# Dense attention of the first layers: a look-ahead that builds up, softmax divisions in two parts, the value bias folded into the output bias, and another pace of the edge work

## What is computed

```python
num_heads = 4; head_dim = C // num_heads; scale = head_dim ** (-0.5); N = H * W
h = _group_norm(x, gn_gamma, gn_beta)
qkv = einsum('oc,bchw->bohw', qkv_w, h) + qkv_b[None, :, None, None]
q, k, v = split(qkv, 3, axis=1)              # each (B, num_heads, head_dim, N)
attn = softmax(einsum('bhdn,bhdm->bhnm', q, k) * scale, axis=-1)
out = einsum('bhnm,bhdm->bhdn', attn, v).reshape(B, C, H, W)
return x + einsum('oc,bchw->bohw', proj_w, out) + proj_b[None, :, None, None]
```

## Time and profile before

| | us |
|---|---|
| median of 3 runs | 2445.96 (2445.37 to 2446.14) |
| the profiled execution | 2440.69 |
| its span, first to last instruction | 2439.0 |
| PE busy, of the span | 1869.7 (77%) |
| DVE busy | 1559.3 (64%) |
| ACT busy | 1039.3 (43%) |
| POOL busy | 719.0 (29%) |
| mean granted TensorE clock | 0.841 of full speed |

### The profile page before, as it was taken

How to read it: one execution, slowest core, us unless ns; L and a number is a source line. 1 busy time by engine, 2 the same in 40 slices (tenths; PEclk the granted TensorE clock), 3 DMA queues, 4 the chain that set the end, 5 groups by cost and what they waited for, 6 DMA issues and landing times. The chain is left out here.

```text
span 2439.0 us, 26403 instructions
## 1 busy us (share of the span) xinstructions
PE 1869.7 (77%) x8810; PEld 846.6 (35%) x8810; DVE 1559.3 (64%) x3609; ACT 1039.3 (43%) x1724; POOL 719.0 (29%) x703
## 2 busy tenths in 40 slices
PE   2966995796688476689957888878878888978494
PEld 1213321321232134456631222222322324864264
DVE  4687777768777685556716575665566554635647
ACT  1333141233314116545533667657656653214255
POOL 3302600630270041024441322332322321127740
PEclk7878897888789787889966999989988986759797
DMA  7002100300120000021001111101011000014100
GB/s 197 1 21 59 44 2 25 77 17 20 50 52 3 25 1 1 1 102 21 14 30 51 42 31 40 41 17 40 29 29 38 3 5 15 1 54 62 10 7 35
DMA packets 55445, 80.16 MB, mean 33 GB/s; under 512 B 17249, under 2 KB 28504, under 8 KB 55073
## 3 DMA queue, kind: packets, MB, share of 16 engines
q1 hardware_dynamic: 44806, 69.14, 9.6%
q10 hardware_dynamic: 6426, 7.99, 1.5%
q0 software_dynamic: 4096, 1.58, 1.4%
HBM read 50.13 MB, written 24.68 MB: 31 GB/s over the span
## 5 line engine op out<-in xcount | busy, mean ns | idle before, releaser
L2460 DVE TENSOR_REDUCE f_half_max<-f_ring 128x1 f32<-128x512 f32 x512 | 334.9, 684 | 272.9 <-PE f_ring L2126 270.8
L2343 ACT ACTIVATE f_probs<-f_ST 128x512 f32<-128x512 f32 x512 | 293.0, 597 | 210.6 <-PE f_ST L2153 206.5
L2126 PE MATMUL f_ring<-f_stacks 96*128 96x512 bf16 x512 | 212.0, 415 | 54.5 <-DVE f_half_max L2460 28.1
L797 DVE TENSOR_REDUCE att_half_max<-att_ring 128x1 f32<-128x512 f32 x256 | 161.1, 683 | 88.1 <-PE att_ring L684 87.0
L2153 PE MATMUL f_ST<-f_stacks 99*128 99x512 bf16 x512 | 204.7, 405 | 10.3 <-ACT f_probs L2343 10.3
L780 ACT ACTIVATE att_probs<-att_ST 128x1024 f32<-128x1024 f32 x128 | 129.3, 1023 | 157.5 <-PE att_ST L709 157.3
L2170 PE MATMUL f_O<-f_probs,f_v_ext 128*32 128x512 f32 x1024 | 154.1, 677 | 0.1
L3182 POOL DMA_INDIRECT ti_row<-features,slot_from x128 | 127.9, 999 | 56.8 <-issue 56.8
L2126 PEld LDWEIGHTS f_ring<-f_stacks 96*128 96x128 bf16 x512 | 50.4, 99 | 258.8 <-DVE f_half_max L2460 162.6
L727 PE MATMUL att_O<-att_probs,v_ext 128*64 128x512 f32 x512 | 134.5, 652 | 6.4 <-DVE att_den L816 6.4
L709 PE MATMUL att_ST<-stacks 96*128 96x512 bf16 (+1 forms) x512 | 137.7, 397 | 0.0
(11 more groups left out here) (588 smaller groups left out, 3507.5 us busy)
## 6 DMA issues: line engine op xcount, KB each, us to landing
f_stacks<-f_parts SPq DMA_DIRECT2D x192, 64.0 KB, 2.2
parts_dram<-l_parts SPq DMA_DIRECT2D x8, 768.0 KB, 3.6
stacks<-parts_dram SPq DMA_DIRECT2D x24, 256.0 KB, 9.7
stacks<-parts_dram ACTq DMA_DIRECT2D x24, 256.0 KB, 10.8
f_parts<-f_parts SPq DMA_DIRECT2D x8, 768.0 KB, 3.5
es_raw<-L_ffn_edge_index SPq DMA_DIRECT2D x8, 512.0 KB, 4.6
bm_mix<-mix SPq DMA_DIRECT2D x8, 512.0 KB, 9.0
xn_cm<-x SPq DMA_DIRECT2D x4, 512.0 KB, 4.2
```

The source lines that it names most:

```text
L797: nc.vector.tensor_reduce(half_max[:, h % 2, t, n:n + 1], ring[:, i % RING], AX.X, ALU.max, negate=True).then_inc(reduced, 1)
L2126: nc.tensor.matmul(ring[:, i % RING], f.stacks[0:STACK, 0, at, t * P:(t + 1) * P], f.stacks[0:STACK, 1, at, n * BANK:(n + 1) * BANK], star ...
L2343: nc.scalar.activation(f.probs[:, s % PROBS, n * BANK:(n + 1) * BANK], ST[:, i % HALVES], ACT.Exp).then_inc(probs_ready, 1)
L2460: nc.vector.tensor_reduce(f.half_max[:, h % 2, t, n:n + 1], ring[:, i % RING], AX.X, ALU.max, negate=True).then_inc(reduced, 1)
```

## The change

In words, in the order of the code:

- `begin`: PE multiplies the output weights with the value bias (one column), and DVE adds the output bias to the result (`k.qb[:, 2:3]`). The sum takes the place of the output bias in the last operation of the attention, and ACT's addition of the value bias to `o_cm` goes.
- `schedule` in `dense_attention`: no scores of the next head at step 0, two tiles (4 products) at steps 1, 2 and 3, one tile from step 4. From step 3 on the same tiles have been made as before. The same in the fifth layer.
- `divide`: the three first heads are divided on 96 rows, in four operations (a reciprocal of one half, its product, the other half) that are taken one a step at steps 26 to 29, ahead of the edge work of that step.
- The last head: `carry_off(3)` goes on both engines. DVE takes one reciprocal of the whole output bank and multiplies 32 rows of numerators with it for either half. PE's output product waits for this alone.
- Edge work: two pieces a step from step 18 instead of from step 22; what would be left after the loop comes behind the last division instead of ahead of it.
- POOL's eight operations wait until the shift parts of head 0 are made.

```diff
@@ begin
+            pe.wait_ge(off, len(order))
+            nc.tensor.matmul(bank_of(0)[:, 0:1], k.turned[:, 3, :], k.cols[:, C_QKV_B + 2:C_QKV_B + 3], start=True,
+                             stop=True).then_inc(folded, 1)
...
+            dve.wait_ge(folded, 1)
+            link(nc.vector.tensor_tensor(k.qb[:, 2:3], bank_of(0)[:, 0:1], k.cols[:, C_PROJ_B:C_PROJ_B + 1], ALU.add))
@@ dense_attention (the same three lines of the schedule in fourth_layer_stream)
+    def ahead(s):
+        return max(min(s + AHEAD, 2 * (s - 1)), 0)
+
...
-        r = s + in_group + AHEAD
-        schedule(s, tiles(in_group if s == 0 else r, r + 1))
+        schedule(s, tiles(in_group + ahead(s), in_group + ahead(s + 1)))
...
+        inverse = c.enter_context(sbuf(nc, "att_inverse", [P, BANK], F32))
...
-                pe.wait_ge(biased, n + 1)
+                pe.wait_ge(normed, NC2 * (groups - 1) + n + 1)
                 nc.tensor.matmul(ring[:, n], w_out, chunk(o_cm, n), start=True, stop=True).then_inc(projected, 1)
...
-            carry_off(groups - 1)
-            for n in range(NC2):
-                act.wait_ge(normed, n + 1)
-                affine(nc, True, chunk(o_cm, n), chunk(o_cm, n), 1.0, bias).then_inc(biased, 1)
...
+            def divide(n):
+                link(nc.vector.reciprocal(den[0:32 * (groups - 1), n * BANK:(n + 1) * BANK],
+                                          den[0:32 * (groups - 1), n * BANK:(n + 1) * BANK]))
+                yield
+                dve.wait_ge(off_by_act, OFF_BY_ACT * (groups - 1))
+                x = o_cm[0:32 * (groups - 1), n * BANK:(n + 1) * BANK]
+                nc.vector.tensor_tensor(x, x, den[0:32 * (groups - 1), n * BANK:(n + 1) * BANK],
+                                        ALU.mult).then_inc(normed, groups - 1)
+                yield
+
+            division = itertools.chain(divide(0), divide(1))
...
+                if s > ends[groups - 2] + visit:
+                    if s == ends[groups - 2] + visit + 1:
+                        dve.wait_ge(off_by_dve, NC2 * (groups - 1))
+                    next(division, None)
                 if beside is not None and s >= EDGES_FROM:
-                    for _ in range(1 if s < in_group + AHEAD + EDGES_FROM - 2 else 2):
+                    for _ in range(1 if s < EDGES_FROM + 4 else 2):
                         next(edge_steps, None)
+            for _ in division:
+                pass
+            dve.wait_ge(mixed_ready, len(steps) // visit)
+            link(nc.vector.reciprocal(inverse[:], O[:]))
+            for n in range(NC2):
+                nc.vector.tensor_tensor(rows_of_group(o_cm, groups - 1, n), O[width * n:width * n + 32, :],
+                                        inverse[width * n + 32:width * (n + 1), :], ALU.mult).then_inc(normed, 1)
             if beside is not None:
                 for _ in edge_steps:
                     pass
-            if share == 1:
-                carry_off(groups - 1)
-                dve.wait_ge(off_by_dve, NC2 * groups)
...
-            for n in range(NC2):
-                link(nc.vector.reciprocal(chunk(den, n), chunk(den, n)))
-                if n == 0 and share == 1:
-                    dve.wait_ge(off_by_act, NC2 * groups)
-                nc.vector.tensor_tensor(chunk(o_cm, n), chunk(o_cm, n), chunk(den, n), ALU.mult).then_inc(normed, 1)
...
+                pool.wait_ge(parts_ready, 1)
                 beside.split(pool, edges_loaded, edges_linked, edges_coded)
@@ finish_attention
-                            chunk(x, n), bank, k.cols[:, C_PROJ_B:C_PROJ_B + 1],
+                            chunk(x, n), bank, k.qb[:, 2:3],
```

More of the change, by code:

```diff
@@ L1871, in fourth_layer_stream @@
     for s in range(len(steps)):
-        r = s + IN_GROUP + f.AHEAD
-        schedule(s, IN_GROUP if s == 0 else r, r + 1)
+        schedule(s, IN_GROUP + ahead(s), IN_GROUP + ahead(s + 1))
         if (s + 1) % NT == 0 and s + IN_GROUP < len(steps):
```

9 lines of the change are left out of this document (4 added, 5 removed).

## The result

The changed kernel takes 2472.3 us (median of 4 runs, 2468.1 to 2479.7), the kernel before 2445.7 (2444.6 to 2446.1): a ratio of 1.0114, 95% interval 1.0096 to 1.0132. It is slower, as forecast, but by 26.6 us instead of 9.0, and outside the range given (2443 to 2461).

A forecast was written before the change was run, and what follows sets the result against it. The limit was taken to change within an attention, DVE's queue setting its end; 9.6 (end) + 2.0 (start) - 2.2 (POOL's wait) - 0.4 (fifth layer) = +9.0 on 2445.96 gave 2455.0 us, range 2443 to 2461.

The forecast's parts named there:

- Part 1: End of each attention: a third reciprocal in DVE's queue outweighs what goes; 2.4 us later an image, +9.6 in all.
- rival 1: Output product: PE at full clock saves 2.0 us an image, giving 2447.1 us, not slower; chance 0.12.
- Part 2: Start of each attention: transposed products start 2.2 us earlier, but maxima gate the first mix; +0.5 an image, +2.0 in all.
- The upper bound: Start of each attention: +1.5 us an image if PE is still at its lower clock by the fourth step.
- Part 3: Head 0's shift parts: POOL's wait ends their collisions with POOL, saving 2.2 us in all.
- Rival 4: Head 1's shift parts: all five operations collide with POOL, +3.6 us an image, 2469 us; chance 0.05.
- Rival 3: Before the last mix: PE at the lower clock becomes the bound, 1 to 4 us an image, 2459 to 2471; chance 0.10.
- Rival 2: Start: maxima don't gate the first mix, so look-ahead gains 2.2 us each start, 2442.4 us; chance 0.13.
- Part 4: Rest: additions in `begin` hidden, folded bias free in the last operation, fifth layer's schedule edit between -2.2 and +1.5, middle -0.4.

The follow-up runs named there:

- the early pieces: Kernel before with folded bias, edge pieces at steps 6 to 29, one a step; with old division 2472.4 us, with new division 2463.2 us.
- the old pace: Changed kernel with edge pieces one a step until step 21 and two from step 22, the new division kept: 2482.4 us.
- the pause alone: Kernel before with folded bias, PE waiting until the first head's shift rows are off ACT before step 0's six scores: 2443.9 us, one execution.
- the pause filled: Changed kernel with two unused products before the first transposed product, 2466.8 us; or with two scores at step 0 instead of none, 2474.1 us.
- the filled pause: Changed kernel with two unused 512-column products between an image's first shift rows and its first transposed product: 2466.8 us.

## Why the prediction was right in sign and wrong in size

**The bill**, as sums over the four attentions of the profiled executions: before 458.1; the folded bias alone 456.2 (-1.9); on top of that the new ending 468.8 (+12.6), the look-ahead 468.1 (+11.9), both without POOL's wait 489.2 (+33.0, 8.5 more than the two by themselves, where three images lose more to head 0's parts and POOL); the whole change 482.7 (+24.6 over before). Cut at the maxima of step 18, 8.8 of the 24.6 lie behind them (forecast 9.6) and 15.8 ahead of them, where parts 2 and 3 had forecast -0.2.

**Part 1, the end: right.** Forecast 48.91 to 51.28 us from the maxima of step 18, +9.6 in all. In image 3 it is 842.61 - 791.41 = 51.20, the last reciprocal starts 833.90 - 791.41 = 42.49 behind those maxima (42.5 forecast), a reciprocal of 96 rows takes 3.35 and that of the output bank 3.36, DVE doesn't wait in between, and PE's last mix ends 3.9 us ahead in image 3 and 5.5 in the others (some 5 forecast). In images 0 to 2 the stretch is 50.9, 51.3 and 51.3. Alone, with the folded bias, the ending cost 10.7, so the sign of the forecast was no luck. That fits the added reciprocal: with the old division and pace DVE has 3.5 us less to do in image 2, and the image is 3.0 shorter; no run takes the reciprocal away by itself. From the output product's start to the attention's end the granted clock was 0.50 in images 1 and 2, 0.67 and 0.57 in 0 and 3, but the product itself was shorter in image 0 alone (PE 3.37 against 3.78): rival 1 came in with 0.4 us.

**Part 2, the start: this step failed.** +2.0 forecast, bounds -2.0 to +6.0; +11.9 measured alone, and in the whole change the first mix comes 2.4 to 3.1 us later in each image, 11.0 in all. The working took the maxima as the gate of the first mix, nine of 0.645 us, and ended with "one score and four products at the faster pitch". In fact PE is the gate: 28 products stand ahead of the first mix in either order, and with the clock low to the end they take 748.62 - 736.23 = 12.39 us, 0.44 each. The price of 0.43 was in the same paragraph, and was used for four of the 28. Before, the clock rose in the middle of them. The upper bound named the case ("still at the lower one by the fourth") but charged one step for it instead of all.

Why the clock rises 7 us later is settled in part. It comes with the order of the products: in twenty images of five kernels with the old order (before, the folded bias alone, the new ending alone, the look-ahead undone, the fifth layer's look-ahead alone) the rise is at 19.5 to 21.5, and at 21 to 23.5 with the early pieces, where head 0's parts met POOL; in twenty of five kernels with the new order (the change, POOL's wait undone, the ending undone, the old pace, the look-ahead alone) it is at 26.5 to 30. With the fifth layer undone it is at 27 to 27.5 in three images and at 23 in one. The pause ahead of it is not the reason, by the run with the pause alone. Why this order does it stays open: PE is busy throughout both, and with the pause filled the rise came at 14.5 to 27.5 from image to image.

**Part 3, POOL's wait: right in what it removes; what it is worth stays open.** Head 0's parts are undisturbed, the counterpart of the earlier trace rows: duration in ns, min/median/max over 16, of which the four longest of L810 are head 1's (the other operations of the five stay under 0.19 us).

```profile
L810 DVE TENSOR_TENSOR att_shift<-att_half_max x16: 166/168/2357, 67.3 to 804.2; 128x8 f32<-128x8 f32 x16
...
L813 DVE CAST att_shift_parts<-att_shift x16: 178/179/181, 67.9 to 804.8; 128x8 bf16<-128x8 f32 x16
```

With the other parts in place, the wait saves 6.5 us of the attentions between two profiled executions, but the medians don't tell it from nothing; forecast 2.2, on collisions as they were before.

**Rival 4** came true in its mechanism and not in its price. In each image one of head 1's five operations waits out POOL's last one:

```profile
754.10 2.36 POOL L2900 TENSOR_TENSOR es_last<-es_last,es_rest 128x1024 f32<-128x1024 f32 x1
754.12 2.36 DVE L810 TENSOR_TENSOR att_shift<-att_half_max 128x8 f32<-128x8 f32 x1
```

It is one and not five as head 1's parts come some 3.4 us later than before, by part 2's loss, when POOL is at its last operation; with the look-ahead undone they come at their old time, and two of the five wait. In image 3 PE then waits 0.63 and 0.30, and the collision costs some 0.6 us an image instead of rival 4's 3.6. The rule of the Trainium skill that the prediction weighed (SBUF — State Buffer, section Who interferes with whom) agrees with these 2.36 us, and with the casts of 2.20 and 2.22 above. Rival 3 did not come at the end of the attention. Rival 2's condition was met, since the first mix doesn't wait for the maxima, but its gain did not come: PE at the lower level is later than they are. Image 0 of the run with the filled pause shows a part of that gain, 1.1 us at the first mix.

**Part 4, the rest: not contradicted for the fifth layer** (-0.4 forecast; the edit alone shows nothing within 0.15%, or 3.7 us, so the size is not shown). "The folded bias costs nothing" is right; in the old ending it even gains. That `begin`'s additions are hidden was not measured by itself.

## What to carry to other kernels

Where a stage begins at the lower clock, add up PE's products at that level all the way to the mark that counts, beside the sum of the engine that seems to gate them; the larger sum is the forecast, unless a trace of that very order shows an earlier rise. Where one engine's queue sets an end, its work counts (an ending with 3.5 us more of it made an image 3.0 longer), and an order that gives it idle time loses. Moving its work up into a stretch that PE bounds is not free: a wait that it causes there cost PE nearly twice its length, by the clock.

## What the hardware showed beyond that

- The same products in the same order, PE without a wait from the shift rows to the rise, had the clock rise 15 us behind an image's start in image 0 and 27 in the next three (two unused products ahead): 114.4 against 120.9 to 121.1 us.
- The fifth layer's attention took 751.5 to 763.5 us in ten profiles in which its program was the same. In the 37.5 us from 337.5 behind its first score the clock was 0.78 in the three longest of them (760.1 to 763.5) and 0.91 in the other seven. Whether the spread of one kernel lies there is not shown. The kernel before, within 1.5 us in four runs at first, spread from 2438 to 2454 in later ones.
- A small DVE operation of 0.17 or 0.18 us takes as long as the rest of the POOL operation beside it (2.36, 2.22, 2.20), and which of the five is hit differs: L810 in the change, L811 and L813 with the look-ahead undone.
